# One gathered step in three blocks fetched row by row from SyncE, in a graph layer on one Trainium2 core

## The reference

```
h = maximum(layernorm(x), 0)
w = edge_weight / maximum(segment_sum(edge_weight, dst), EPS)[dst]
feat = relu(h @ W_pool + b_pool)
neigh = segment_max(feat[src] * w, dst);  neigh = where(deg > 0, neigh, 0)
rst = h @ W1_self + neigh @ W1_neigh + b1
h2 = relu(rst / maximum(norm(rst), EPS))
neigh2 = segment_sum(h2[src] * w, dst) / maximum(deg, 1)
out = x + relu(h2 @ W2_self + neigh2 @ W2_neigh + b2)
```

## Time and profile before

| | us |
|---|---|
| median of 2 runs (4083.5 to 4085.26) | 4084.38 |
| the profiled execution | 4083.49 |
| its span | 4081.8 |
| POOL busy | 3053.1 (75%) |
| DVE busy | 3065.1 (75%) |
| PE busy | 2858.1 (70%) |
| ACT busy | 1348.3 (33%) |

### The profile page before, as it was taken

One profiled execution on the slowest core, in us unless ns is written; L12 is line 12 of the kernel. 1 busy time (PEld: TensorE's weight loads), 2 busy tenths in 40 slices (PEclk: granted clock), 3 DMA queues, 4 the chain that ended last, 5 costly groups with the idle time before them and its releaser, 6 DMA issues. The chain is left out here.

```text
span 4081.8 us, 32603 instructions
## 1 busy us (share of the span) xinstructions
PE 2858.1 (70%) x8603; PEld 1431.6 (35%) x8603; DVE 3065.1 (75%) x5592; ACT 1348.3 (33%) x4000; POOL 3053.1 (75%) x3238
## 2 busy tenths in 40 slices
PE   4033342222399999992679999999999999998536
PEld 3033232222244444441433333333333333345324
DVE  6477797877688888883568888888888888875224
ACT  6344443333333333332533333333332332333310
POOL 7777777777777777776767777777777777777766
PEclk8555555555599999996579999999999999997555
DMA  7233334444433333333433333333333333333335
GB/s 207 86 110 110 106 118 128 125 125 125 137 108 107 118 108 115 110 107 107 103 95 107 117 107 107 120 107 107 117 107 118 107 109 115 107 105 114 104 113 146
DMA packets 206127, 468.14 MB, mean 115 GB/s; under 512 B 57362, under 2 KB 122900, under 8 KB 181108
## 3 DMA queue, kind: packets, MB, share of 16 engines
q0 software_dynamic: 103232, 211.68, 19.9%
q1 hardware_dynamic: 102708, 254.37, 17.3%
HBM read 240.76 MB, written 225.06 MB: 114 GB/s over the span
## 5 line engine op out<-in xcount | busy, mean ns | idle before, releaser
L448 POOL DMA_INDIRECT G<-h_tab,SRC x1495 | 1410.6, 944 | 467.9 <-issue 401.1
L448 POOL DMA_INDIRECT G<-feat_tab,SRC x1443 | 1368.3, 948 | 439.8 <-issue 379.1
L770 DVE TENSOR_TENSOR CP<-pH,kc 128x1024 f32<-128x1024 f32 x1225 | 1494.5, 1220 | 94.0 <-PE pM L928 55.4
L547 ACT ACTIVATE pT<-G,EW 128x128 f32<-128x128 f32 x1522 | 550.1, 368 | 1173.5 <-DMA G<-h_tab,SRC 532.4
L547 ACT ACTIVATE pM<-G,EW 128x128 f32<-128x128 f32 x1416 | 503.7, 367 | 1239.9 <-DMA G<-feat_tab,SRC 559.0
L903 PE MATMUL pH<-CP 128*128 128x98 bf16 x1563 | 144.5, 281 | 604.1 <-DVE CP L728 604.1
L927 PE MATMUL pM<-CP,A 128*128 128x512 f32 x882 | 467.4, 612 | 72.8 <-DVE CP L770 72.3
L928 PE MATMUL pM<-CP,A 128*128 128x512 f32 x882 | 455.4, 598 | 0.0
L927 PE MATMUL pC<-CP,A 128*128 128x512 f32 x784 | 413.9, 610 | 55.5 <-DVE CP L770 55.4
L713 DVE SCALAR_TENSOR_TENSOR S<-S,C,pT 128x128 f32<-128x128 f32 x782 | 270.2, 346 | 240.2 <-ACT pT L547 221.3
L928 PE MATMUL pC<-CP,A 128*128 128x512 f32 x784 | 403.1, 596 | 0.0
(11 more groups left out here) (146 smaller groups left out, 2858.9 us busy)
## 6 DMA issues: line engine op xcount, KB each, us to landing
scan<-S SPq DMA_DIRECT2D x97, 1032.0 KB, 4.3
scan<-S SPq DMA_DIRECT2D x97, 1024.0 KB, 4.1
G<-h_tab,SRC POOLq DMA_INDIRECT x1495
G<-feat_tab,SRC POOLq DMA_INDIRECT x1443
CP<-in_srcq SPq DMA_DIRECT2D x25, 256.0 KB, 5.5
feat_tab<-F SPq DMA_DIRECT2D x24, 256.0 KB, 2.4
h_tab<-A SPq DMA_DIRECT2D x24, 256.0 KB, 2.6
U<-in_x SPq DMA_DIRECT2D x24, 256.0 KB, 3.8
```

The lines of the kernel that those rows point to most:

```text
L448: pool.indirect_dma_start(out=dst, out_offset=None, in_=table, in_offset=bass.IndirectOffsetOnAxis(ap=idx, axis=0)).then_inc(s, 16)
L547: act.activation(scaled(t), v, ACT.Copy, scale=EW[:, t:t + 1]).then_inc(s_mul, 1)
L770: dve.tensor_tensor(OH[:, k % 2, :, :], pH[:, :].unsqueeze(1).to_broadcast([P, 2, 4 * P]), kc[:, 2 * j:2 * j + 2].unsqueeze(2).to_broadcas ...
```

## The change

One step in every three blocks (steps 57, 105, ... 1545: `ROWT`, 32 in each phase, 64 in all) is taken out of POOL's order. SP fetches its 128 rows instead, each with a DMA of its own of 512 bytes, into one of two new buffers `GR`. The row numbers come as a new input `srcr`, one row per fetched step; SP loads it once into `IX`, DVE turns it into byte offsets with one shift by 9, and SP reads 16 offsets at a time into registers (`sp.load`) and issues 16 DMAs with them. These 8 pieces per step are spread over the three blocks: 2, 3 and 3 of them at the heads of the blocks, ahead of each block's store. Before the first piece SP waits until the step that used the buffer before (two fetched steps back) has been multiplied. ACT's `multiply` waits for 128 rows on `s_row` instead of for a gather. The number of semaphores that the early gathers from x rotate over falls from 32 to 16 (`NX`).

```diff
-NX = 32
+NX = 16
...
+RB = 3
+RL = 16
+CH = P // RL
+NGS = 2
+ROWT = [T * RB * (k + 1) + 9 for k in range((NB - 1) // RB)]
+NROW = len(ROWT)
+RAT = {(phase, t): phase * NROW + k for phase in range(2) for k, t in enumerate(ROWT)}
+ROWORD = list(RAT)
...
-GORD = [(0, t) for t in SEQ if (0, t) not in PAT] + [(1, t) for t in range(TS) if (1, t) not in PAT]
+GORD = [(0, t) for t in SEQ if (0, t) not in PAT and (0, t) not in RAT] + \
+    [(1, t) for t in range(TS) if (1, t) not in PAT and (1, t) not in RAT]
...
+        GR = sb("GR", [P, NGS, D])
+        IX = sb("IX", [P, P], I32)
...
+                    sp.dma_start(IX[:, :], srcr).then_inc(s_ixl, 16)
...
+            flat = [tab.rearrange("n d -> (n d)").bitcast(U8) for tab in (feat, htab)]
+
+            def fetch_rows(phase, c):
+
+                k, i = phase * NROW + c // CH, c % CH
+                if c == 0:
+                    if phase == 0:
+                        sp.wait_ge(s_ix, 1)
+                        all_done(sp, s_fst, NGR)
+                    else:
+                        all_done(sp, s_hst, NGR)
+                if i == 0 and k >= NGS:
+                    ph, before = ROWORD[k - NGS]
+                    sp.wait_ge(s_mul, ph * TS + before + 1)
+                regs = [sp.alloc_register(f"row{k}_{i}_{r}") for r in range(RL)]
+                sp.load(regs, IX[k:k + 1, i * RL:(i + 1) * RL])
+                for r in range(RL):
+                    p = i * RL + r
+                    at = sp.snap(regs[r], donate=True)
+                    sp.dma_start(GR[p:p + 1, k % NGS, :].bitcast(U8),
+                                 flat[phase][bass.ds(at, 4 * D)].rearrange("(a d) -> a d", a=1))\
+                        .then_inc(s_row[k % NGS], 16)
...
+                    for c in range(CH * b // RB, min(CH * (b + 1) // RB, CH * NROW)):
+                        fetch_rows(phase, c)
                     sp.wait_ge(s_cmb, phase * TS + r[-1] + 1)
...
+                elif (phase, t) in RAT:
+                    k = RAT[phase, t]
+                    act.wait_ge(s_row[k % NGS], 16 * P * (k // NGS + 1))
+                    v = GR[:, k % NGS, :]
...
+                    dve.wait_ge(s_ixl, 16)
+                    dve.tensor_scalar(IX[:, :], IX[:, :], 9, None, ALU.logical_shift_left).then_inc(s_ix, 1)
```

More of the change, by code:

```diff
@@ L53 @@
 PAT = {(QUADS[u][0], t): (u, i) for u in range(QN) for i, t in enumerate(quad_steps(u))}
-GORD = [(0, t) for t in SEQ if (0, t) not in PAT] + [(1, t) for t in range(TS) if (1, t) not in PAT]
+RB = 3
[6 more added lines that the diff above has]
+ROWORD = list(RAT)
+assert all(t < TS and t not in XAT and (phase, t) not in PAT for phase, t in RAT)
+GORD = [(0, t) for t in SEQ if (0, t) not in PAT and (0, t) not in RAT] + \
+    [(1, t) for t in range(TS) if (1, t) not in PAT and (1, t) not in RAT]
 LT = 8
@@ L78 @@
 I32 = mybir.dt.int32
+U8 = mybir.dt.uint8
 def tiles_of(g):
@@ L108, with build @@
 OWN = own_rows()
-def build(nc, x, src, srcq, dstx, ew, w_pool, b_pool, w1s, w1n, b1, w2s, w2n, b2, out):
+def build(nc, x, src, srcq, srcr, dstx, ew, w_pool, b_pool, w1s, w1n, b1, w2s, w2n, b2, out):
     feat = nc.dram_tensor("feat_tab", (NP, D), F32).ap()
@@ L242, in build @@
         s_xg = [sem(f"s_xg{i}") for i in range(NX)]
+        s_row = [sem(f"s_row{i}") for i in range(NGS)]
+        s_ixl = sem("s_ixl")
+        s_ix = sem("s_ix")
         s_mul = sem("s_mul")
@@ L1005, in _ @@
             node_stage(1, s_y)
-_NAMES = ["x", "src", "srcq", "dstx", "ew", "w_pool", "b_pool", "w1s", "w1n", "b1", "w2s", "w2n", "b2"]
+_NAMES = ["x", "src", "srcq", "srcr", "dstx", "ew", "w_pool", "b_pool", "w1s", "w1n", "b1", "w2s", "w2n", "b2"]
 def kernel(x, src, dst, edge_attr_128, edge_weight, L0_gnn_W_pool, L0_gnn_b_pool, L0_gnn_W1_self,
@@ L1027 @@
     srcq = np.stack([srcs[:, list(quad_steps(u))].T.reshape(-1) for u in range(QN)])
-    given = [filled(x, 0, NP, 0), srcs[:, order], srcq, dstx, filled(edge_weight, 0, EP, 0),
+    srcr = filled(np.stack([srcs[:, t] for _, t in ROWORD]), 0, P, 0)
+    given = [filled(x, 0, NP, 0), srcs[:, order], srcq, srcr, dstx, filled(edge_weight, 0, EP, 0),
              L0_gnn_W_pool, L0_gnn_b_pool, L0_gnn_W1_self, L0_gnn_W1_neigh, L0_gnn_b1,
```

## The result

The changed kernel takes 4311.89 us (4310.84 to 4312.93), the kernel before 4084.38: a ratio of 1.056, with a 95% interval of 1.051 to 1.060. The forecast was 4004, and the range ended at 4260. It is wrong, and to the other side; the time is that of the rivals in which SyncE becomes the bound.

What follows compares the result with a forecast made beforehand. The prediction took POOL's count of back-to-back gathers as the bound: 4084.4 us less 80.1 for 64 gathers gave 4004.3 us, with everything else, SP's added work included, costed at nothing. The range was 3998 to 4260 us.

Steps and rivals of the forecast that it cites:

- POOL sets the time: Edge phases: POOL's gathers run back to back at about 1.25 us each; 32 fewer in each phase save 80.1 us.
- What lies beside the path: DVE's shift, SP's 64 KB load, the smaller `NX` and ACT's other semaphore: costed at nothing, under 2 us without cover.
- TensorE and DVE in the quads: Quads: picks take 83.8 us of a quad's 92.8 after the change, DVE 88 of 100; both fit, costed at nothing.
- DMA traffic: DMA engines: 8,192 added packets of 512 bytes cost at most 901 us of one engine, 22%; it fits.
- SP's sum for three blocks: SP's queue: 128 row DMAs at 0.30, 8 register loads at 1.0 and stores make 47.5 us, bounds 37.5 and 75.7.
- g: SP's queue: its time in us for three blocks, forecast at 47.5; up to 57.3 the kernel stays within 2%.
- The room in each stage: Time SP has for three blocks: 58.7 us in the plain stage, 48.7 in the lean stage, 55.7 in the quads.
- the formula for the loss: All stages: 11 x (g - 48.7) + 42 x (g - 55.7) + 12 x (g - 58.7) us, each where positive.
- Rival C: SP's queue: slow register loads make SP the bound everywhere; at 2.8 us a load, 4447 us; chance 0.13.
- rival D: SP's queue: a row DMA addressed from a register costs like a full tile, 0.47 us, giving 4929 us; chance 0.11.
- Where the wait shows: Signs of a slow SP: DVE's first step waiting for a store, ACT's multiply for rows, SP's `s_cmb` waits gone.

Runs made afterwards that it cites:

- h1: The changed kernel with row addresses written into the program and no register loads: 4007.99 us against 4084.01 for the kernel before, ratio 0.982.
- e5: The changed kernel without SP's row fetches, fetched steps reading zeros: 5062.18 us against 5141.95 for the kernel before, ratio 0.985, on the slower chips.
- f1: The changed kernel with each block's first register load ahead of the store's wait, no lean-stage fetched steps: 4088.99 us against 4091.35 for the kernel before.

## Why the prediction was wrong

**POOL sets the time, 80.1 us to gain:** right. h1 has 76 of them.

**What lies beside the path (shift, load of `IX`, `NX`, ACT's wait):** right, by h1 and e5. **TensorE and DVE in the quads** fit, as h1 shows with 76 of the 80 us. **DMA traffic:** right; gathers are 944 and 948 ns in h1 as in the earlier trace rows.

**SP's sum for three blocks, 47.5 us:** this is the step that failed. It measured 59.6. The register load, L, was 1.99 us against 1.0, which makes 7.9, and the row DMA, c, 0.332 against 0.30, which makes 4.1. Of c's miss, the address from a register is most: rows from registers are 0.322 us apart in the median, rows from fixed addresses 0.295. The value for L was the middle of two rows that have nothing to do with a register load, and its upper bound, 1.8, was below the mean measured. It also took the loads as free of what stands ahead of them, while 3 of 8 stand behind a 1 MB store and take 3.1 us (3.4 to 4.0 where one of the other loads stands between). Neither miss alone leaves the range: by the prediction's formula, L = 1.99 alone gives g = 55.4 and 4078 us, c = 0.332 alone g = 51.6 and 4036. Together they take SP over the room of all three stages.

**The room in each stage and the formula for the loss:** right. With g = 59.6 it gives 4004 + 11 x 10.9 + 42 x 3.9 + 12 x 0.9 = 4299 us, 13 below the measured. Rival C has the mechanism, slow register loads with SP as the bound everywhere, but not the size: g did cross its 57.3 us, while L, 1.99, stayed under its 2.2; it took the dearer row as well, and the price of 4447 was for L = 2.8. In rival D the row DMA cost 0.47; it did not.

**Where the wait shows:** half right. I expected the store behind the rows to hold DVE and ACT. It was the rows that came late, and ACT's multiply that held everything.

The Trainium skill's page "DMA: Bandwidth & Descriptors", section "Latency and other measured facts", has a floor of about 600 ns for a register load; the shortest here, 1.15 us for 16 registers, lies above it. The 200 ns a register of the Trainium skill's page "Runtime: NRT & Kernel Launch", section "Instruction fetch mechanics", would make 3.2 us of 16 registers, an estimate. The loads right behind a store come near that, at 3.1, but those between rows take 1.26, and one register more costs 0.054: the rule does not hold for these loads, which read SBUF.

## What to carry to other kernels

An engine that waits 3600 us of 4082 is not free for 8,192 small jobs: work out its time per period against the shortest period of any stage, price by price, and where one price is unseen, let it decide the chances, not a middle value. A helper with room in every stage (62 of 65.4 us at the tightest) gives nearly all of the gain; at 102 to 122% of its time it becomes the bound and takes back more than the gain; taking fewer jobs (one step in four blocks) gave 1.4% on the chips of level 1, where one in three cost 5.6%, and on those of level 2 even that lost 12%. Count the instructions that an issue from a register really makes, and look at what stands ahead of each: a load of 1.26 us between rows was one of 3.1 behind a store.

## What the runs showed of the hardware

- DMAs of one 512-byte row each leave SyncE 0.322 us apart when the address comes from a register (a MOVE of 0.029, the DMA 0.228 and the gaps), and 0.295 apart when it is written in the program (0.252 and a gap of 0.04), both in the median.
- A load of 16 registers from SBUF takes SyncE 1.26 us between such rows and about 3.1 right behind the issue of a 1 MB store; 32 registers take 2.12 and 3.8 (on the chips of level 2). With the load moved away, the first four rows behind the store are slow instead, up to 1.10 us each in f1 and 1.41 in h1, 1.2 to 1.4 us more in sum.
- 8,192 extra DMAs of one row each left the gathers of GpSimd at 944 to 948 ns.
- The same kernel took 4084 us on some chips and over 5050 on others, with pauses between instructions of SyncE and ScalarE where nothing was waited for; the kernel with 17,366 instructions on SyncE took 4312 and 6559.
